# Gated feed-forward on one core: routing logits by 8 products of 32 columns, halves added on VectorE, routed bias by one product

## The reference

```python
scores = softmax(xf @ gate_w.T)                    # 16 experts
orig, scores = scores, scores + gate_b
group_scores = top_k(scores.reshape(T, 4, 4), 2)[0].sum(-1)
keep = the 2 best of the 4 groups; idx = the 2 best experts within them
combine = (one_hot(idx) * orig[idx][..., None]).sum(1)
h = silu(xf @ We1[e] + be1[e]) * (xf @ We3[e] + be3[e])     # 64 wide, each expert
y = sum_e combine[:, e] * (h @ We2[e] + be2[e])
z = the same with the shared weights ws1, ws3, ws2, 128 wide, without routing
x = x + 0.5 * (y + z)
```

## Time and profile before

| what | us |
|---|---|
| median of three runs | 3306.5 |
| lowest and highest of the three | 3298.94, 3322.9 |
| the profiled execution: its own time | 3298.4 |
| the profiled execution: its span | 3296.6 |
| mean granted TensorE clock, share of full | 0.914 |
| PE, DVE, ACT, POOL busy, share of the span | 88%, 76%, 54%, 28% |

### The profile page before, as it was taken

One profiled execution on the slowest core, in us unless ns is written; L12 is line 12 of the kernel. 1 busy time (PEld: TensorE's weight loads), 2 busy tenths in 40 slices (PEclk: granted clock), 3 DMA queues, 4 the chain that ended last, 5 costly groups with the idle time before them and its releaser, 6 DMA issues. The chain is left out here.

```text
span 3296.6 us, 46625 instructions
## 1 busy us (share of the span) xinstructions
PE 2901.1 (88%) x15938; PEld 1755.8 (53%) x15938; DVE 2512.6 (76%) x6115; ACT 1769.9 (54%) x2711; POOL 927.4 (28%) x885
## 2 busy tenths in 40 slices
PE   6999959999999997999976688899799999989753
PEld 4767623444344433667754556566565656556432
DVE  6888777888888871888867897777366688797765
ACT  3444306777777776444445555454344555555544
POOL 2222021211221101122201454565223333334233
PEclk9999958999999998999985788989899999999875
DMA  4444422122122111343420000000000000000000
GB/s 129 91 91 93 89 100 94 69 83 95 54 94 97 55 50 56 80 102 85 98 52 1 1 14 20 13 20 26 26 14 14 14 14 7 14 7 26 7 7 26
DMA packets 71588, 167.20 MB, mean 51 GB/s; under 512 B 8792, under 2 KB 9400, under 8 KB 67128
## 3 DMA queue, kind: packets, MB, share of 16 engines
q1 hardware_dynamic: 69176, 160.03, 16.8%
q10 hardware_dynamic: 2176, 4.19, 0.3%
HBM read 120.67 MB, written 43.52 MB: 50 GB/s over the span
## 5 line engine op out<-in xcount | busy, mean ns | idle before, releaser
L706 DVE TENSOR_REDUCE att_mx<-att_pair 128x2 f32<-128x1024 f32 x512 | 617.5, 1221 | 133.9 <-PE att_pair L955 133.6
L881 ACT ACTIVATE att_pt<-att_pair 128x1024 f32<-128x1024 f32 x512 | 522.1, 1025 | 216.2 <-PE att_pair L965 213.0
L977 PE MATMUL att_o<-att_pt,att_vx 128*32 128x256 f32 x4096 | 324.8, 402 | 10.7 <-ACT att_oT L887 5.8
L955 PE MATMUL att_pair<-att_k,att_q 24*128 24x512 f32 x1024 | 272.4, 536 | 49.0 <-DMA att_k<-att_spread_k 14.2
L965 PE MATMUL att_pair<-att_q,att_k 26*128 26x512 f32 x1024 | 259.8, 507 | 0.0
L965 PEld LDWEIGHTS att_pair<-att_q,att_k 26*128 26x128 f32 x1024 | 96.7, 187 | 186.9 <-issue 160.7
L955 PEld LDWEIGHTS att_pair<-att_k,att_q 24*128 24x128 f32 x1024 | 100.6, 195 | 136.7 <-ACT att_pt L881 89.9
L457 ACT ACTIVATE ffnA_h<-ffnA_up,b 128x512 f32<-128x512 f32 x144 | 98.4, 685 | 135.8 <-PE ffnA_up L105 135.3
L457 ACT ACTIVATE ffnB_h<-ffnB_up,b 128x512 f32<-128x512 f32 x144 | 98.5, 685 | 134.4 <-PE ffnB_up L105 133.9
L1897 ACT ACTIVATE att1k_sq<-att1k_k 128x512 f32<-128x512 f32 x128 | 76.2, 595 | 168.4 <-PE att1k_k L105 165.9
L977 PEld LDWEIGHTS att_o<-att_pt,att_vx 128*32 128x32 f32 x4096 | 90.6, 110 | 138.7 <-issue 116.7
(11 more groups left out here) (538 smaller groups left out, 7770.3 us busy)
## 6 DMA issues: line engine op xcount, KB each, us to landing
ffnA_weights<-ffnA_weights SPq DMA_DIRECT2D x128, 256.0 KB, 5.3
att_q<-att_spread_q SPq DMA_DIRECT2D x16, 1024.0 KB, 5.0
att_k<-att_spread_k SPq DMA_DIRECT2D x16, 1024.0 KB, 4.8
att_spread_q<-att_qhi SPq DMA_DIRECT2D x32, 256.0 KB, 2.5
att_spread_k<-att_khi SPq DMA_DIRECT2D x32, 256.0 KB, 3.3
twk_hi<-ffnB_weights SPq DMA_DIRECT2D x32, 256.0 KB, 4.0
twk_lo<-ffnB_weights SPq DMA_DIRECT2D x32, 256.0 KB, 5.1
tgk_hi<-ffnB_weights SPq DMA_DIRECT2D x32, 256.0 KB, 6.0
```

The source lines that it names most:

```text
L706: v.tensor_reduce(top[b % 2][:, t, h:h + 2], pair("s", k)[:, :].rearrange("p (h n) -> p h n", h=2), AX, ALU.max, negate=True).then_inc(mx, 1)
L881: a.activation(pt[k % 8][:, :, :].rearrange("p h n -> p (h n)"), pair("t", k)[:, :], ACT.Exp, scale=scale).then_inc(p_, 1)
L955: last = pe.matmul(pair("s", k)[:, (j - j0) * 512:(j - j0 + 1) * 512], qb[b % 3][r, u, t * P:(t + 1) * P], kb[b % 3][r, u, :], start=True, ...
L977: last = pe.matmul(obank[j * BLOCK:(j + 1) * BLOCK, cols], vxb[b % 3][:, t, 4 * u + j, :], pt[(2 * g + j // 2) % 8][:, j % 2, cols], start ...
```

## The change

The high and low parts of the gate weights now lie side by side in one tensor of 48 columns: low, high, and 16 columns of zeros. A product of xh with the first 32 columns and one of xl with the last 32 add up, for each tile, to two halves of 16 columns: xh times low plus xl times high, and xh times high. That is 8 products with 32 moving columns for a group. VectorE adds the halves (one TENSOR_REDUCE over a view that puts the two last, from PSUM into r["s"]), and the maximum and the subtraction read r["s"]. A new semaphore `sum` joins them, and frees `lt` for TensorE in place of `sh`.

For the routed bias, W["b2"] is one tensor with be2's high part in rows 0 to 31 and its rest in rows 32 to 47, and `combT` gets row 32 to 47, the float32 weights rounded, as well. One product then sums all parts. The transfer of be2 is 48 rows, not 32. In `setup0` two small operations more run on VectorE.

```diff
@@ class Ffn0Signals @@
-         self.up3, self.sil, self.gl, self.plain, self.kept, self.hc, self.dn, self.y, self.yo, self.add) = signals(
+         self.up3, self.sil, self.gl, self.plain, self.kept, self.hc, self.dn, self.y, self.yo, self.add, self.sum) = signals(
@@ ffn0, vector, gate(i) @@
-            lg = ltb[:, 0:TILES * EXPERTS].rearrange("p (t e) -> p t e", t=TILES)
+            parts = ltb[:, 0:2 * TILES * EXPERTS].rearrange("p (t k e) -> p t e k", t=TILES, k=2)
             v.wait_ge(S.lt, i + 1)
-            m = st.at(v.tensor_reduce(r["mx"], lg, AX, ALU.max))
+            v.tensor_reduce(r["s"], parts, AX, ALU.add).then_inc(S.sum, 1)
+            yield
+            v.wait_ge(S.sum, i + 1)
+            m = st.at(v.tensor_reduce(r["mx"], r["s"], AX, ALU.max))
             yield
             v.wait_ge(st.sem, m)
-            v.tensor_tensor(r["e"], lg, bc16(r["mx"]), ALU.subtract).then_inc(S.sh, 1)
+            v.tensor_tensor(r["e"], r["s"], bc16(r["mx"]), ALU.subtract).then_inc(S.sh, 1)
@@ ffn0, scalar, combined(i) @@
-            a.activation(combT[i % 2][0:32, :], combb[0:32, :], ACT.Copy).then_inc(S.ct, 1)
+            a.activation(combT[i % 2][0:48, :], combb[0:48, :], ACT.Copy).then_inc(S.ct, 1)
@@ ffn0, tensor, gate(i) @@
-                pe.wait_ge(S.sh, i)
+                pe.wait_ge(S.sum, i)
             for t in range(TILES):
-                last = pairs3(pe, ltb[:, t * EXPERTS:(t + 1) * EXPERTS], [p[:, t * P:(t + 1) * P] for p in x], [w[:, :] for w in W["gate"]])
+                tokens, out = slice(t * P, (t + 1) * P), ltb[:, t * 2 * EXPERTS:(t + 1) * 2 * EXPERTS]
+                pe.matmul(out, x[0][:, tokens], W["gate"][:, 0:2, :].rearrange("p k e -> p (k e)"), start=True, stop=False)
+                last = pe.matmul(out, x[1][:, tokens], W["gate"][:, 1:3, :].rearrange("p k e -> p (k e)"), start=False, stop=True)
@@ ffn0, tensor, down(n) @@
-                pe.matmul(acc[:, :], W["b2"][0][:, :], combT[i % 2][:, :], start=True, stop=False)
-                pe.matmul(acc[:, :], W["b2"][1][:, :], combT[i % 2][:, :], start=False, stop=False)
+                pe.matmul(acc[:, :], W["b2"][:, :], combT[i % 2][:, :], start=True, stop=False)
@@ setup0, vector @@
-        split(v, st, W["gate"][0][:, :], W["gate"][1][:, :], small("gate"))
-        split(v, st, W["b2"][0][:, :], W["b2"][1][:, :], b2[:, :])
+        split(v, st, W["gate"][:, 1, :], W["gate"][:, 0, :], small("gate"))
+        st.at(v.memset(W["gate"][:, 2, :].bitcast(F32), 0.0))
+        high = slice(2 * EXPERTS, 3 * EXPERTS)
+        m = st.at(v.tensor_copy(b2_high[high, :], b2[high, :]))
+        m = st.at(v.tensor_copy(W["b2"][:, :], b2[:, :]))
+        v.wait_ge(st.sem, m)
+        st.at(v.tensor_tensor(W["b2"][high, :], b2[high, :], b2_high[high, :].bitcast(F32), ALU.subtract))
```

More of the change, by code:

```diff
@@ L175, in ffn0_tensors @@
     return {"w1": pair("w1", [P, CHUNKS, P]), "w3": pair("w3", [P, CHUNKS, P]), "w2": sb("w2", [P, CHUNKS, P]),
-            "b13": sb("b13", [P, 2, CHUNKS]), "bs2": sb("bs2", [P, 1]), "b2": pair("b2", [P, P]),
-            "small": sb("small", [P, SMALLS]), "gate": pair("gate", [P, EXPERTS]), "gate_b": sb("gate_b", [P, EXPERTS])}
+            "b13": sb("b13", [P, 2, CHUNKS]), "bs2": sb("bs2", [P, 1]), "b2": sb("b2_parts", [P, P], F32R),
+            "small": sb("small", [P, SMALLS]), "gate": sb("gate_parts", [P, 3, EXPERTS], F32R), "gate_b": sb("gate_b", [P, EXPERTS])}
 ROUTING = (("e", 16), ("prob", 16), ("s", 16), ("pm", 8), ("psum", 8), ("gsum", 4), ("alt", 4), ("gs", 4), ("g1", 4),
@@ L206, in __init__ @@
         (self.var, self.root, self.xn, self.xT, self.xh, self.xl, self.lt, self.sh, self.ex, self.comb, self.cT, self.ct, self.up1,
-         self.up3, self.sil, self.gl, self.plain, self.kept, self.hc, self.dn, self.y, self.yo, self.add) = signals(
-            nc, ctx, name, "var root xn xT xh xl lt sh ex comb cT ct up1 up3 sil gl plain kept hc dn y yo add")
+         self.up3, self.sil, self.gl, self.plain, self.kept, self.hc, self.dn, self.y, self.yo, self.add, self.sum) = signals(
+            nc, ctx, name, "var root xn xT xh xl lt sh ex comb cT ct up1 up3 sil gl plain kept hc dn y yo add sum")
         self.cw = signals(nc, ctx, name, "cw0 cw1 cw2 cw3")
@@ L1072, in setup0 @@
     b2, bvw = mem.sb("raw_b2", [P, P]), mem.sb("bvw", [P, C])
+    b2_high = mem.sb("b2_high", [P, P], F32R)
     spread = mem.sb("spread", [P, CHUNKS - 1, P])
@@ L1101, in sync @@
         sp.wait_ge(zero, 1)
-        load(b2[0:2 * EXPERTS, :], d["L0_b2"])
+        load(b2[0:3 * EXPERTS, :], d["L0_b2"])
         load(W["w2"][:, :, :].rearrange("p c i -> p (c i)"), d["L0_w2"])
@@ L2526, in laid_out @@
     out["L0_w2"] = by_chunks(np.concatenate([f0("We2").reshape(-1, C), f0("ws2")]))
-    out["L0_b2"] = np.concatenate([f0("be2"), f0("be2")])
+    out["L0_b2"] = np.concatenate([f0("be2"), f0("be2"), f0("be2")])
     out["L0_qkv"] = spread_heads(a0("qkv_w"))
```

## The result

Over 20 runs each, the changed kernel has a median of 3297.64 us and the kernel before one of 3317.91; the ratio is 0.9946 with a 95% interval of 0.9924 to 0.9967. That is 0.54% faster, clear of noise and within the 1% that the prediction drew as its line. The saving by the medians is 20.3 us; the forecast had 20.6. The interval allows a saving of 11 to 25 us.

The account below looks back on a forecast made before the run. TensorE's instructions, one behind another, were taken to bound the steady groups. Two stages of 10.5 us each, 21.0, less 0.35 in setup0, gave 20.6 us off the median of 3306.5: 3285.9 us, range 3268 to 3308.

Parts of the forecast that it names:

- What bounds the steady part: Steady groups of ffnA and ffnB: TensorE has no idle time, so its instructions set the 23.42 us a group.
- The logits: TensorE, each group: four of 12 products go at 0.111 us each, saving 0.445 us a group.
- The routed bias: TensorE, each group: one product goes, saving 0.235 us; ScalarE's copy of 48 rows instead of 32 costs nothing.
- VectorE's operation: VectorE, each group: the added reduction costs 0.32 us, bounds 0.25 and 1.25, hidden in idle time.
- The cover: VectorE's idle time hiding the reduction: 0.26 us left ahead of chunk 5's silu, then 0.75 ahead of line 286.
- Rival (a): VectorE's place ahead of chunk 5's silu becomes the bound if the reduction exceeds 0.58 us; about 3305 us; chance 0.09.
- The first group: Start of each stage: four fewer logits save 0.53 us, bounds 0 and 0.60; TensorE's wait grows to 5.1 us.
- setup0: Setup ahead of the stages: two more VectorE operations cost 0.35 us once, bounds 0 to 0.6.
- Sum: Whole kernel: two stages save 21.0 us, less 0.35 in setup0, so 20.6 us; forecast chance 0.66.
- The other side (b): TensorE's clock in untouched stages: 0.01 lower costs up to 28 us; chance 0.09 slower, 0.07 clearly faster.

Follow-up runs that it names:

- e1: The changed kernel with the routed bias given back its two products, so only the logits change stays: ffnA 382.0 us, ratio of the whole 0.9949.
- e8: The changed kernel with 128 moving columns in each of the eight logits products, 96 of them zeros: pace 0.11 us, ffnA 377.5 us.
- e9: The changed kernel with eight more products a group behind the logits, 64 weight and 32 moving columns: 0.059 us each, ffnA 385.5 us.
- e2: The kernel before with only the routed bias changed to one product, logits as before: ffnA 385.3 us, ratio of the whole 0.9964.
- e6: The changed kernel with VectorE's addition of the halves done four times, extra ones into scratch tiles: a steady group stays 22.74 us.
- e7: The changed kernel with VectorE's addition done seven times, extra ones into scratch tiles: twelve steady groups of ffnA take 22.88 us in the mean.

## Why the prediction was right

- **What bounds the steady part.** Right: TensorE has no idle time from 60 to 380 us before or after, and 22.74 us a group were forecast and measured.
- **The logits.** 0.111 us each at 32 columns, four fewer: right, shown alone by e1 (382.0 for 382.1 us). The prediction read the pace off 16 and 66 columns without a reason; e8 and e9 give one, the 128 weight columns.
- **The routed bias.** 0.235 us a group: right, shown alone by e2. The copy of 48 rows takes 0.59 us, as the one of 32 does.
- **VectorE's operation.** 0.32 us forecast, 0.32 measured. The cover was right in size, 0.26 + 0.75 = 1.01 forecast and 1.10 measured, and wrong in place. The step "the idle time shrinks from 1.26 to 0.26 us" failed: none is left ahead of chunk 5, because the later step moved the work before `c_sum`, and the idle time gathered ahead of chunk 6. The order that was shown with the change held this; I read of it only the place where the operation was added. Rival (a), which took the first of the two idle times as the limit, fell with e6 and e7.
- **The first group.** The wait came as forecast (5.01 for 5.1 us). Its gain, 0.53 us a stage with 0.60 as the upper bound, can't be read from one pair of profiles. From the first logits product to the transposes of the weights the first pair gives 1.15 us less in ffnA (18.49 to 17.34) and 0.20 less in ffnB (18.14 to 17.94), but the kernel before, run again, took 17.53 and 17.64, and the changed one 17.09 and 17.76. The means of four are 17.95 and 17.53, 0.42 less; with e2 beside the one and e1 beside the other it is 0.53. That is the size forecast, within a spread of 0.96 us in one kernel. The spread goes with how long TensorE's pace stays slow at the start of a stage: its products of 512 columns start 0.43 us apart there and 0.235 later, and the first at the fast pace comes 8.8 and 8.4 us behind the first logits product before (6.4 and 6.6 again), 6.5 and 8.0 after (6.0 and 7.8 again), later where the stretch is longer. Why it differs stays open. The kernel before in ffnA, first and again (columns as in the earlier trace rows):

```profile
22.86:41.35 18.49, 14.12 (x58) 11.95 (x58) 11.12 (x46) 5.58 (x8) 1.64 (x3) 0.91 0.00 0
23.25:40.78 17.53, 13.17 (x58) 11.25 (x58) 11.04 (x46) 5.58 (x8) 1.66 (x3) 0.97 0.00 0
```

- **setup0.** 0.35 us forecast. From `setup_bvw` to the last operation it took 12.16 - 11.05 = 1.11 us before and 12.95 - 11.34 = 1.61 after: 0.50. ffnA's first product came 0.78 later in the first pair; the other 0.28 is a transfer that ended later, and the kernel before itself has that product at 22.86 and, run again, at 23.25.
- **Sum.** 11.0 + 9.9 - 0.5 = 20.4 us from the stages of the first pair of profiles, 10.2 + 9.5 - 0.5 = 19.2 from the second, 20.3 from the medians, 20.6 forecast. The stages bear the sum out within 1.4 us; that the medians meet it within 0.3 is luck, since their interval is 11 to 25 us.
- **The other side (b).** Its mechanism is real, in attn0 alone: between two runs of the kernel before attn0 fell from 0.92 to 0.85 and the stages behind ffnB kept 0.88. The mean of the two stretches in the earlier trace rows fell by 0.025 with this, and the span grew by 46.6 us, 19 us for each 0.01. So the price, up to 28 us, held as a bound, and the swing was larger than the 0.01 that I weighed. It strikes both kernels, so it moves single times and widens the interval of the ratio; nothing shows that it favours one kernel.

## What to carry to other kernels

Where one engine has no idle time in a long steady stretch, read the pace of the instructions to be removed from start to start, multiply by the groups, and compare stages by their lengths in the profile rather than whole times: here a stage repeats within 0.9 us, a steady group within 0.02, and the whole within 62. A gain below 1 us at the start of a stage needs several profiles of each kernel. Small products that load new weights each time cost their weight columns: with 128 of these, products of 16, 32, 66 and 128 moving columns all passed at 0.11 us, so widen the moving side to have fewer of them. Before an operation is added to an engine with little idle time, add up all its idle time in a period, and look in the order at what each later step moves past.

## What the runs showed that was not expected

The clock of TensorE in attn0 varies between launches of one program: 0.92 and 0.85 granted, 887.4 and 938.6 us, with 815 to 868 us busy. Nearly all the spread between runs of this kernel, 3288.56 to 3350.18 us, may come from there: attn0 grew by 51.2 us where the span grew by 46.6 in the kernel before, and by 30.6 where it grew by 29.5 in the changed one. Why the clock falls in one launch and not in another stays open. Reductions of one shape that do not depend on each other started 0.20 us apart on VectorE, where the one that needs their result started 0.32 us behind.
